# The layer norm and output tail of the last expert's token tiles, deferred behind the first matmul pass of the next tile

## The reference, cut to what matters

```python
h = jax.nn.gelu(jnp.einsum('nd,edh->enh', xf, w1) + b1[:, None, :], approximate=False)
y = jnp.einsum('enh,ehd->end', h, w2) + b2[:, None, :]
...
out = jnp.einsum('nk,nkd->nd', gates, y_sel - c_sel + c_sum[None, None, :])
...
x = _layernorm(x + out_of_ffn, axis=-1)      # D = 1024, hidden 4096, 4 experts, 2 chosen
```

## Time and profile before

| | us |
|---|---|
| runs (2) | 8949.88 and 8387.3, median 8668.59 |
| the profiled execution | 8300.43 |
| its spans, cores 0 to 3 | 8238.9 to 8241.3 |
| its spans, cores 4 to 7 | 8258.7 to 8298.9 |

### The profile page before, as it was taken

One profiled execution on the slowest core, in us unless ns is written; L12 is line 12 of the kernel. 1 busy time (PEld: TensorE's weight loads), 2 busy tenths in 40 slices (PEclk: granted clock), 3 DMA queues, 4 the chain that ended last, 5 costly groups with the idle time before them and its releaser, 6 DMA issues.

```text
span 8298.9 us, 87148 instructions; the slowest of 8 cores (8238.9 to 8298.9 us)
## 1 busy us (share of the span) xinstructions
PE 6049.7 (73%) x31972; PEld 3149.6 (38%) x31972; DVE 1452.4 (18%) x4211; ACT 1538.1 (19%) x4214; POOL 244.7 (3%) x387
## 2 busy tenths in 40 slices
PE   1347677736767772499998999989999777777777
PEld 1213333312333331234443444433444355555555
DVE  1103233320333331300000000000000022222222
ACT  0012222211222221111211112111211121222222
POOL 0000000000000000000000000000000000000000
PEclk9975665558566555699998999999999876777778
DMA  3259500025700003000002111132111311111101
GB/s 69 95 93 115 88 24 16 19 76 117 97 31 23 15 20 104 6 31 22 25 31 97 31 21 26 31 97 31 20 27 31 97 35 36 36 36 36 36 31 38
DMA packets 200965, 396.07 MB, mean 48 GB/s; under 512 B 14662, under 2 KB 121358, under 8 KB 193126
## 3 DMA queue, kind: packets, MB, share of 16 engines
q0 software_dynamic: 37504, 155.22, 12.3%
q1 hardware_dynamic: 119394, 176.49, 6.4%
q10 hardware_dynamic: 43656, 58.80, 2.3%
HBM read 339.98 MB, written 193.07 MB: 64 GB/s over the span
## 4 chain that ended last, share of the span: by engine, by line
PE 66%; DMA 15%; DVE 9%; issue 6%; ACT 2%; another core or an unknown queue 1%; DVEq 1%; SPq 0%; ACTq 0%; POOL 0%; POOLq 0%
PE psC L237 28%; PE psA L237 26%; PE psD L237 6%; PE psB L235 5%; DMA w2sb<-sw2bf 2%; DMA x1c_b<-sx 2%; DMA x1t_a<-sx1bf 2%; DMA xn<-x 2%; DMA xr<-sx 1%; DVE big_scr L519 1%; DMA y<-out_b 1%; DVE ztmp L674 1%; DMA sx<-xe 1%; DVE big_scr L517 1%; DVE PT L604 1%
## 5 line engine op out<-in xcount | busy, mean ns | idle before, releaser
L237 PE MATMUL psA<-x1t_a,w1sb 128*128 128x512 bf16 x6144 | 1381.8, 389 | 43.0 <-ACT hT_a L1061 43.0
L237 PE MATMUL psC<-hT_a,w2sb 128*128 128x512 bf16 x6144 | 1336.4, 380 | 23.6 <-ACT hT_a L1061 19.5
L1061 ACT ACTIVATE hT_a<-psA,b1c 128x512 bf16<-128x512 f32 x768 | 527.6, 687 | 2505.3 <-PE psA L237 2309.0
L237 PEld LDWEIGHTS psA<-x1t_a,w1sb 128*128 128x128 bf16 x6144 | 611.1, 100 | 838.0 <-issue 148.7
L237 PEld LDWEIGHTS psC<-hT_a,w2sb 128*128 128x128 bf16 x6144 | 600.9, 98 | 757.6 <-issue 42.1
L237 PE MATMUL psC<-PT,v_all 64*64 64x128 bf16 (+1 forms) x2048 | 357.8, 276 | 314.3 <-DVE ztmp L674 268.7
L237 PE MATMUL psC<-hT_b,w2sb 128*128 128x256 bf16 x4096 | 524.3, 295 | 79.2 <-DMA x1c_b<-sx 78.8
L1090 DVE SCALAR_TENSOR_TENSOR ctr_a<-psC,ccols,mb_a 128x512 f32<-128x512 f32 x192 | 144.2, 751 | 2421.3 <-PE psC L237 2352.8
L237 PE MATMUL psA<-x1t_b,w1sb 128*128 128x256 bf16 x4096 | 521.6, 296 | 6.2 <-ACT hT_b L1061 6.1
L237 PEld LDWEIGHTS psC<-hT_b,w2sb 128*128 128x128 bf16 x4096 | 424.2, 105 | 178.9 <-issue 103.5
L237 PEld LDWEIGHTS psA<-x1t_b,w1sb 128*128 128x128 bf16 x4096 | 413.5, 105 | 119.9 <-issue 22.6
(11 more groups left out here) (152 smaller groups left out, 4727.6 us busy)
## 6 DMA issues: line engine op xcount, KB each, us to landing
sacc<-ctr_a POOLq DMA_DIRECT2D x192, 256.0 KB, 4.1
sw1bf<-w POOLq DMA_DIRECT2D x8, 4096.0 KB, 86.9
sw2bf<-w POOLq DMA_DIRECT2D x8, 4096.0 KB, 123.9
w1sb<-sw1bf SPq DMA_DIRECT2D x32, 1024.0 KB
w2sb<-sw2bf ACTq DMA_DIRECT2D x32, 1024.0 KB
x1t_a<-sx1bf SPq DMA_DIRECT2D x24, 1024.0 KB
xn<-x SPq DMA_DIRECT2D x32, 512.0 KB
sx<-xe SPq DMA_DIRECT2D x64, 256.0 KB
```

What stands on the lines that cost most here:

```text
L237: return E_.matmul(o, l, r, start=st, stop=sp)
L1061: gl_last = sop(lambda s, hc=hc, i=i, e=e: s.activation(hT[:, TW * hc:TW * hc + TW], psA[i][:, 0:TW], AF.Gelu, bias=b1c[e][:, hc:hc + 1], ...
```

## The change

In the last expert, the code from the layer norm to the stores of `y` becomes a function, which is put on a list. It is called one tile later: after GEMM1 of the next tile has been emitted (and after the constant pass `c_pass`, which exists for the first tile alone), before that tile's GEMM2. The last tile's function is called after the loop. The function's instructions are the same, with the same tiles and banks. `rt_ready`, the token for the end of the joins, is fixed when the function is made; all counts that are read at emission are read when it is called.

```diff
+        pend_ln = []
         for tt in range(n_tt):
...
             if tt == 0:
                 t_cpass = c_pass(e)
+            if last_e and pend_ln:
+                pend_ln.pop(0)()
             for dc in range(8):
...
             if last_e:
                 rt_ready = [("s_dve", P.cnt["s_dve"])] * 8
-                r2t = [big_scr[:, TW * dc:TW * dc + TW] for dc in range(8)]
-                ln_done = layer_norm(rt_ready, r2t, TW=TW)
-                for tc4 in range(ntc):
...
-                    rout[i].free = t_o
-                rbig.free = ("s_pe", P.cnt["s_pe"])
+
+                def ln_out_tail(tt=tt, rt_ready=rt_ready):
+                    r2t = [big_scr[:, TW * dc:TW * dc + TW] for dc in range(8)]
+                    ln_done = layer_norm(rt_ready, r2t, TW=TW)
+                    for tc4 in range(ntc):
...
+                        rout[i].free = t_o
+                    rbig.free = ("s_pe", P.cnt["s_pe"])
+                pend_ln.append(ln_out_tail)
+        if last_e:
+            while pend_ln:
+                pend_ln.pop(0)()
```

More of the change, by code:

```diff
@@ L1143, in ffn_expert @@
-                rbig.free = ("s_pe", P.cnt["s_pe"])
+                def ln_out_tail(tt=tt, rt_ready=rt_ready):
+                    r2t = [big_scr[:, TW * dc:TW * dc + TW] for dc in range(8)]
+                    ln_done = layer_norm(rt_ready, r2t, TW=TW)
+                    for tc4 in range(ntc):
+                        i = tc4 % 2
+                        for g in range(2):
+                            tok = None
+                            for j in range(4):
+                                dc = 4 * g + j
+                                tok = mm(psB32[g][:, 128 * j:128 * j + 128],
+                                         big_scr[:, TW * dc + 128 * tc4:
+                                                 TW * dc + 128 * tc4 + 128],
+                                         ident32[:, :], j == 0, j == 3,
+                                         waits=wl(rB[g].free, ln_done[dc])
+                                         if j == 0 else [ln_done[dc]],
+                                         transpose=True,
+                                         inc="s_pe" if j == 3 else None)
+                            t_ev = vop(lambda v, g=g, i=i: v.tensor_copy(
+                                out_sb[i][:, 512 * g:512 * g + 512],
+                                psB32[g][:, 0:512]),
+                                waits=wl(tok, rout[i].free if g == 0 else None))
+                            rB[g].free = t_ev
+                        row0 = TW * tt + 128 * tc4
+                        t_o = dma_store(y[row0:row0 + 128, :], out_sb[i][:, :],
+                                        waits=[("s_dve", P.cnt["s_dve"])])
+                        rout[i].free = t_o
+                    rbig.free = ("s_pe", P.cnt["s_pe"])
```

## The result

The changed kernel is faster by 1.7%: the ratio to the kernel before is 0.983, 95% interval 0.9766 to 0.9893, and in a second session 0.9802 (0.9683 to 0.992). Its five fastest runs lie at 8094.79 to 8097.88 us, the four fastest of before at 8237.08 to 8265.73; the best runs are 142 us apart. Forecast were 124 us, 1.5%. The median over all 11 runs is 8201.81 us, forecast 8263 in a range of 8140 to 8590.

The account below looks back on a forecast made before the run. Bound taken: in each seam the tail and the next tile's loads stand one after the other. 141 us saved less 17 for the clock gives 124, off the faster run's 8387.3: 8263 us, range 8140 to 8590.

Parts of the forecast that it names:

- The seam: From a tile's GEMM2 to the next tile's GEMM1: falls from 35.36 to 7.1 us, upper bound 8.1.
- The gap: Between GEMM1 and GEMM2 of a tile: grows from 2.61 to 21.5 us, holding the whole tail.
- Rival B: The tail runs hidden beside GEMM1, between-pass wait stays 2.6 us: 424 us saved, 7876 or 7963; chance 3%.
- What was costed at nothing: Second `out_b` copies end 2.6 us into GEMM2, VectorE's first join comes after 4.1: cover 1.5 us, no cost.
- The clock: GEMM2 also starts at half clock: 1.75 us per tile, 0.6 given back, net 1.15, 17 us in 15.
- rival A: GEMM2 stays at half clock: 20.9 us more per tile against 9.4 saved, 8473 or 8560; chance 4%.
- rival C: Denser order puts the other half of core 5's tiles at 0.81 clock: 64 us saved, 8236 or 8323; chance 10%.
- Rival D: Stores or load still hold GEMM1, 12.2 us or more before it: 47 us saved, 8253 or 8340; chance 3%.

Follow-up runs that it names:

- the run with added matmuls: Changed kernel plus 54 matmuls per tail whose results are not read, to hold the clock: one run, 8074.97 us, beside 8105.38 for the changed kernel.
- two buffers: Changed kernel with two `x1t` buffers and two gate rows, the next tile's load emitted behind GEMM1: ratio 0.9685, best run 8006.68 us.
- the kernel with all three: Changed kernel plus two `x1t` buffers, the tail spread inside GEMM1, and GEMM2's w2 wait counting only w2 loads: best runs 7775.39 and 7757.89 us.
- the kernel with two tails in flight: Against the kernel with all three: Ln, Exp behind last Gelu, normalisation inside GEMM2, transposes in next GEMM1; best 7683.59 and 7673.34 us.

## Why the prediction was right, point by point

- **The seam.** 7.1 us forecast, 101.48 / 15 = 6.77 measured. The 0.3 us that I added for the sacc pieces beside the load did not come: 3.92 us from the load's issue to the gate row's (7599.86 to 7603.78), 4.15 before.
- **The gap.** 21.5 us forecast, 315.81 / 15 = 21.05 measured. The whole tail stands in it, in the order that the queues of ScalarE and TensorE impose. Rival B was excluded by that, and what it would have taken to get it was another order of emission.
- **What was costed at nothing.** The copies end 3.5 us into GEMM2 (2.6 forecast); 0.5 us of the difference is a longer wait for the first store (3.33 us instead of 2.80); why it took longer was not tried. The cover was 0.9 us, not 1.5. It held, but closely.
- **The clock.** This is the term that was mis-sized most, and 13 of the 20 us by which core 0's stretches beat the forecast's 124 are its; the other 7 are seam and gap, each a little shorter than forecast. Forecast: one more slow start, net 1.15 us per tile. Measured on core 0: GEMM1 +0.42, GEMM2 −0.14, together +0.28; on cores 0 to 3 together +0.24 and +0.27, 0.5 us. Two things failed in it. The cost of a slow start was read from GEMM1, which starts after idle time; GEMM2 starts right behind the transposes, and its slow start costs about 0.9 us, as the run with added matmuls shows. And what GEMM2 paid already was read on core 5, where 6 tiles of 15 do; on core 0 it is 11, so that more was given back there than the 0.6 I took. On one tile of the changed kernel the three stretches are: the tail from the end of the sums, the first 3.4 us of GEMM2, the rest of it:

```profile
7642.50:7658.58 16.08, 8.34 (x24) 4.51 (x24) 9.29 (x23) 2.52 (x5) 0.00 (x0) 0.51 0.08 25
7658.58:7662.00 3.42, 3.42 (x28) 2.81 (x27) 1.29 (x2) 0.00 (x0) 0.00 (x0) 0.82 0.29 117
7662.00:7691.00 29.00, 25.39 (x231) 22.13 (x229) 9.75 (x21) 0.00 (x0) 3.77 (x7) 1.00 0.24 74
```

  GEMM2 is back at 1.00 within 3.5 us here, and no GEMM2 of core 0 has a mean below 0.94. That also settles rival A. The rule of the Trainium skill ("TensorE: Matmul & The Clock Gate", section "HAM oscillation — how this bites in real kernels"), that each stall is paid anew, held for the seam: though it fell from 35.0 to 6.8 us, GEMM1's slow start stayed, and it went only with the seam itself (30.8 to 29.4 us with two buffers). The start of one GEMM1 of the changed kernel:

```profile
7606.23:7610.03 3.80, 3.60 (x17) 2.19 (x16) 0.42 (x1) 1.82 (x3) 0.00 (x0) 0.50 0.00 0
```

- **The lower clock of a busy die (rival C).** Not seen to follow the order. In the changed kernel no pass of core 0 is below 0.91. In the densest kernel, with 65 us per tile, all eight cores had a mean clock of 1.00 over the same 936 us, with TensorE busy for 97% of them; here core 0:

```profile
6712.00:7648.00 936.00, 910.30 (x7930) 751.84 (x7930) 323.84 (x735) 326.40 (x728) 63.29 (x118) 1.00 0.18 57
```

  So the rule quoted beside this rival, which ties the third level to three cores of a die in dense matmuls at once, did not show in this execution. What sets the 0.81 of core 5 before was not tried. The rival's idle time is misread as well: 9.4 us are a quarter of seam and gap, but a third of TensorE's idle time, 26.9 us per tile by the earlier trace rows.
- **Rival D.** The load leaves the queue 0.2 us after GEMM2. Excluded.
- **The absolute time.** Forecast 8263, median 8201.81. That this lies in the range is luck: the same kernel's median in the second session was 8481.88, while its best runs were 11 us apart. The scale came from two runs of the kernel before, 8387.3 and 8949.88, of which neither is near its best, 8237.08. What the prediction can be held to is the difference.
- **What I had not worked out** is that the deferral wasn't needed. A gain of this size can be had from one queue's order, and the tail in its old place gives 1.8 us per tile more, because GEMM2 then follows its Gelus after 2.7 us and the load runs under the tail. The prediction said that the load and the tail "stand one after the other that need not", but costed only the way in which the change parts them.

## What to carry to other kernels

Moving a serial chain behind a dense pass hides nothing if its instructions stand behind the pass in every queue: look at what each in-order queue holds ahead of the chain's first instruction. The gain of this change lay in another queue, in a load that no longer stands behind two stores, and could be had alone. To hide the chain itself, cut it up among the blocks, and keep the part that switches ScalarE's tables where TensorE doesn't need ScalarE.

## What the runs showed of the hardware

- A stop of 2.99 us of TensorE in the midst of dense matmuls brought the granted clock to 0.56 over the 9 us around and behind it. Behind the gap of 2.6 us of the kernel before GEMM2 began at half clock in 6 to 11 of 15 tiles, depending on the core. A stop of 3.64 us inside one GEMM2 of the run with added matmuls left 0.69 over the 8 us around it. The stops inside the GEMM2 shown from 6852.09 on, the longest 1.20 and 1.58 us, left the clock at 1.00. Without gap and stops GEMM2 fell by 5.7 us, though its stops were only some 3.8 us (33.79 less 29.97 busy).
- The price of a slow start depends on what stands ahead of it: 1.75 us for GEMM1 behind a load by the earlier trace rows, of which its removal gave back 1.4; about 0.9 us for GEMM2 behind transposes; and 1.3 us for the tail's own chain at half clock.
- The table load ahead of Ln took 1.28 us as before and Ln followed it at once. The Trainium skill ("ScalarE: Activation LUTs", section "What ACT_TABLE_LOAD costs") adds a drain of 1380 ns to each switch. The trace shows none between the load and its neighbours: in the kernel with all three the first load ends at 7177.01 and Ln starts at 7177.02, Exp ends at 7177.94 and the second load starts at 7177.96.
- Eight cores in dense matmuls at once, each busy for 97% of 936 us, ran at a granted clock of 1.00 throughout in the profile of the kernel with two tails in flight. In the kernel before, core 5 had whole passes at 0.81.
